# GpSimd handles both channel halves of a scan state in one instruction

## The reference

```
x = x + 0.5 * ffn(layernorm(x))     # 8 routed experts (top 2) + 2 shared experts
x = x + ssm(layernorm(x))           # selective state-space scan
x = x + 0.5 * ffn(layernorm(x))     # the same experts again
```

```
h[d,n] = exp(dt[d] * A[d,n]) * h[d,n] + dt[d] * B[n] * x[d]
y[d]   = sum over n of h[d,n] * C[n]  +  D[d] * x[d]
```

## Time and profile before

| | |
|---|---|
| three runs, us | 519.59, 522.36, 525.29 |
| span of the profiled execution (first to last instruction), us | 517.8 |
| VectorE busy, us | 324.0 (63%) |
| ScalarE busy, us | 158.6 (31%) |
| GpSimd busy, us | 231.4 (45%) |
| chain that ended last | PE 90%, DVE 6%, DMA 2% |
| scans with the tiles beside them | about 158 to 243 us and 296 to 380 us |

### The profile page before, as it was taken

The page is one execution under the profiler, slowest core; times in us unless marked ns, Lnnn a source line. Parts: engine busy times, 40 slices in busy tenths (PEclk is TensorE's granted clock), DMA queues, the critical chain, the costliest instruction groups (busy, mean ns, idle before and its releaser), DMA issues.

```text
span 517.8 us, 11713 instructions
## 1 busy us (share of the span) xinstructions
PE 506.7 (98%) x4666; PEld 423.2 (82%) x4667; DVE 324.0 (63%) x658; ACT 158.6 (31%) x337; POOL 231.4 (45%) x208
## 2 busy tenths in 40 slices
PE   8998999999999999999989999999999899999997
PEld 6998996568979999557979799975598899955696
DVE  3844338123747999997679399999967532422225
ACT  1111122221156434553203643445521111122210
POOL 1051000602216999995454289999920650000032
PEclk9999999999999999999999999999999999999999
DMA  7958999512415455541322445545200231210012
GB/s 231 392 231 303 394 389 346 178 59 66 129 36 142 118 139 135 163 117 30 113 63 71 129 94 121 156 131 155 73 22 2 72 101 52 82 42 14 20 54 81
DMA packets 42232, 67.91 MB, mean 131 GB/s; under 512 B 5152, under 2 KB 24992, under 8 KB 42176
## 3 DMA queue, kind: packets, MB, share of 16 engines
q1 hardware_dynamic: 29424, 38.94, 26.5%
q10 hardware_dynamic: 9088, 18.09, 9.4%
q0 software_dynamic: 3664, 10.10, 6.1%
HBM read 48.89 MB, written 18.22 MB: 130 GB/s over the span
## 4 chain that ended last, share of the span: by engine, by line
PE 90%; DVE 6%; DMA 2%; issue 1%; ACT 0%; POOL 0%; DVEq 0%; POOLq 0%; ACTq 0%
PE ps L526 40%; PE ps L551 20%; PE ps L541 14%; PE ps L564 7%; PE ps L570 2%; PE ps L575 2%; PE ps L707 2%; DMA bcb<-bc_rows 1%; PE ps L718 1%; PE ps L748 1%; DVE hb L1054 1%; DMA bc_rows<-hh 1%; DVE hb L1058 0%; PE ps L609 0%; PE ps L759 0%
## 5 line engine op out<-in xcount | busy, mean ns | idle before, releaser
L526 PEld LDWEIGHTS ps<-xt,w_gu 128*128 128x128 f32 x1400 | 161.6, 192 | 5.7 <-issue 3.8
L526 PE MATMUL ps<-xt,w_gu 128*128 128x128 f32 x1400 | 163.8, 276 | 0.4 <-DVE xres L1069 0.4
L1054 DVE SCALAR_TENSOR_TENSOR hb<-hb,ps 128x640 f32<-128x640 f32 x68 | 55.4, 815 | 121.3 <-ACT hb L800 121.2
L551 PE MATMUL ps<-w_dn,hb 128*128 128x256 f32 x520 | 120.8, 380 | 0.0
L551 PEld LDWEIGHTS ps<-w_dn,hb 128*128 128x128 f32 x520 | 94.8, 190 | 10.8
L800 ACT ACTIVATE hb<-ps 128x640 f32<-128x640 f32 x68 | 47.6, 700 | 176.9 <-PE ps L526 163.0
L526 PE MATMUL ps<-xnt,w_gu 128*128 128x128 f32 x680 | 80.5, 276 | 3.0 <-DVE xres L1069 2.7
L1099 DVE TENSOR_TENSOR_SCAN ps<-ps,region 128x512 f32<-128x512 f32 x64 | 78.3, 1223 | 8.1 <-POOL region L1018 6.2
L1032 POOL TENSOR_TENSOR xnt<-xnt,hh 128x512 f32<-128x512 f32 x64 | 82.2, 1286 | 2.5 <-DVE hh L1104 2.5
L526 PEld LDWEIGHTS ps<-xnt,w_gu 128*128 128x128 f32 x680 | 78.7, 192 | 5.5 <-DVE xres L1069 3.1
L998 POOL DMA_INDIRECT region<-yg_rows,ypos x32 | 30.5, 954 | 110.2 <-DMA yg_rows<-ob 88.4
(11 more groups left out here) (112 smaller groups left out, 302.0 us busy)
## 6 DMA issues: line engine op xcount, KB each, us to landing
bcb<-bc_rows SPq DMA_DIRECT2D x22, 512.0 KB, 5.1
region<-bc_rows SPq DMA_DIRECT2D x10, 512.0 KB, 5.0
w_gu<-in_wg ACTq DMA_DIRECT2D x7, 640.0 KB, 9.8
xg<-xg_rows SPq DMA_DIRECT2D x35, 128.0 KB, 4.2
w_gu<-in_wu ACTq DMA_DIRECT2D x7, 640.0 KB, 11.2
w_dn<-in_wd ACTq DMA_DIRECT2D x7, 640.0 KB, 13.8
yg_rows<-ob SPq DMA_DIRECT2D x20, 128.0 KB, 3.5
xg_rows<-bcb SPq DMA_DIRECT2D x1, 2176.0 KB, 14.9
```

The source lines that it names most:

```text
L526: last = nc.tensor.matmul(gup(p)[:, c * P:(c + 1) * P], w_gu4[:, e, k, c * P:(c + 1) * P], x, start=(k == 0), stop=(k == KC - 1))
L551: ins = nc.tensor.matmul(outp(p), hb[:, p, c * P:(c + 1) * P], w_dn4[:, e, c, :], start=(c == 0), stop=(c == IC - 1))
L1054: nc.vector.scalar_tensor_tensor(out=h, in0=h, scalar=1.0, in1=gup(p)[:, 0:I], op0=ALU.add, op1=ALU.mult).then_inc(s_a, 1)
```

## The change

GpSimd's two passes take both channel halves in one instruction of 128 partitions by 1024 elements: 16 inputs and 16 adds to a scan where there were 32 and 32. The input reads B once and spreads it over the two halves with a step of 0. bx exists twice, by even and odd state (the new one is `bx1`, 4 KB of each partition), and input m waits for the scans of state m-2. To make room, GpSimd's ring for DMA descriptors is set to 8 KB of each partition. VectorE's instructions stay as they are, 32 scans and 32 products; but a scan waits for the input of the whole state, and a product of state m for the add of the whole state m-1. TensorE's step Y counts 16 adds.

```diff
+        bx1 = sb("bx1", [P, KC, HALF])
...
-        bx = region[:, 1024:2048].rearrange("p (d t) -> p d t", d=KC)
+        bx = [region[:, 1024:2048].rearrange("p (d t) -> p d t", d=KC), bx1[:, :, :]]
...
-                    pe.wait_ge(s_acc, (h + 1) * HALVES)
+                    pe.wait_ge(s_acc, (h + 1) * N)
...
-                    def input_of(g):
-                        m, d = g // KC, g % KC
+                    def input_of(m):
                         pool.wait_ge(s_bcl[m % SLOTS], 16 * slot_loads(h, m))
-                        if m > 0:
-                            pool.wait_ge(s_scan, HALVES * h + g - KC + 1)
-                        nc.gpsimd.tensor_tensor(bx[:, d, :], dtx[:, d, :], bcs[m % SLOTS][:, 0, :],
-                                                ALU.mult).then_inc(s_bx, 1)
-
-                    for g in range(KC):
-                        pool.wait_ge(s_dtx, KC * h + g + 1)
-                        input_of(g)
-                    for g in range(HALVES):
-                        d = g % KC
-                        if g + KC < HALVES:
-                            input_of(g + KC)
-                        pool.wait_ge(s_hc, HALVES * h + g + 1)
-                        if g == 0:
+                        if m > 1:
+                            pool.wait_ge(s_scan, HALVES * h + KC * (m - 1))
+                        nc.gpsimd.tensor_tensor(bx[m % 2], dtx[:, :, :], bcs[m % SLOTS][:, 0:1, :]
+                                                .to_broadcast([P, KC, HALF]), ALU.mult).then_inc(s_bx, 1)
+
+                    pool.wait_ge(s_dtx, KC * (h + 1))
+                    input_of(0)
+                    input_of(1)
+                    for m in range(N):
+                        pool.wait_ge(s_hc, HALVES * h + KC * (m + 1))
+                        if m == 0:
                             pool.wait_ge(s_skip, h + 1)
-                        pool.wait_ge(s_acc, HALVES * h + max(g - KC + 1, 0))
-                        nc.gpsimd.tensor_tensor(xnt[:, d, :], xnt[:, d, :], hh[:, d, :], ALU.add).then_inc(s_acc, 1)
+                        else:
+                            pool.wait_ge(s_acc, N * h + m)
+                        nc.gpsimd.tensor_tensor(xnt[:, :, :], xnt[:, :, :], hh[:, :, :], ALU.add).then_inc(s_acc, 1)
+                        if m + 2 < N:
+                            input_of(m + 2)
...
-                    dve.wait_ge(s_bx, HALVES * h + g + 1)
-                    nc.vector.tensor_tensor_scan(state_banks[:, d, :], state_banks[:, d, :], bx[:, d, :], 0.0,
+                    dve.wait_ge(s_bx, N * h + m + 1)
+                    nc.vector.tensor_tensor_scan(state_banks[:, d, :], state_banks[:, d, :], bx[m % 2][:, d, :], 0.0,
...
                     if m > 0:
-                        dve.wait_ge(s_acc, HALVES * h + g - KC + 1)
+                        dve.wait_ge(s_acc, N * h + m)
...
-    nc = bacc.Bacc("TRN2", target_bir_lowering=False, num_devices=1)
+    nc = bacc.Bacc("TRN2", target_bir_lowering=False, num_devices=1, dynamic_dma_scratch_size=8192)
```

## The result

The change takes 548.39 us (median of 4 runs, 546.15 to 549.82), the kernel before in the same comparison 521.78 us (4 runs, 519.59 to 525.29): a ratio of 1.0511, 95% interval 1.0457 to 1.0565. The forecast was 549.4 us, range 541 to 556. The profiled execution took 546.15 us with a span of 544.2, 26.4 more than the span before.

A forecast was written before the change was run, and what follows sets the result against it. TensorE, busy 506.7 of 517.8 us, was taken as the bound; VectorE's new waits for whole adds, with start and end, make each scan 13.5 us longer, together +27.0 on the median 522.36: 549.4 us, range 541 to 556.

The forecast's parts named there:

- the named states: VectorE's product waits for the add before states 1, 2, 5, 6, 9, 10, 12, 13, 15: 13.1 us a scan.
- six covered: At six of 15 changes of state, a tile's hidden values stand between products on VectorE: no wait below T of 2.59.
- T: Time of a 1024-element GpSimd instruction, taken as 2.46 us; VectorE's wait without hidden values is T - 1.00.
- the sum: One scan's start, nine waits, exponentials' idle times and end: Y 13.5 us later, 11 us for each us of T.
- The later start: The first scan needs the input of both halves, so it starts at 160.42 instead of 159.23: +1.19 us.
- Y waits for the last add: At a scan's end TensorE reaches Y at about 255.2, but the last add lets Y start at 256.21.
- the ring: The smaller descriptor ring costs nothing: gathers start 1.25 us apart and land in 2.8, about three under way.
- the whole inputs and their step of 0: GpSimd's inputs between states cost nothing; the next add is held up only if an input takes over 2.7 us.
- the loads of B and C: Issued at the second product of m-1, landing 5.1 us later, needed over 7 us after it: no cost.
- A sign of being wrong that did show: The prediction is wrong if TensorE, now idle in places, is granted a clock of less than 1.00.
- Not slower: Rival: one GpSimd instruction is far cheaper than two, T below 1.47, at most +5.2 us for both scans; 6 in 100.
- slower still: Rival: GpSimd becomes the bound through slow inputs, or the halved ring holds gathers back: 556 us and more; 8 in 100.

The follow-up runs named there:

- run 5: The change with other shares of half-states to the 12 tiles: 546.58 us, the kernel before 525.52.
- run 8: The change with the input of state m+2 ahead of the add of state m on GpSimd's list: 590.71 us, the kernel before 525.52.
- run 4: The change with a second hh buffer, by even and odd state: 527.65 us, the kernel before 523.15.
- run 7: The change with adds as two instructions of 512, both behind both products of the state: 531.38 us, the kernel before 525.52.
- run 1: The kernel before with the descriptor ring at 8 KB and nothing else: 522.75 us, the kernel before 523.15.
- run 6: The kernel before with other shares of half-states to the 12 tiles: 535.07 us, the kernel before with its own shares 525.52.
- run 2: The change with adds by half, a product waiting for its own half's add, inputs whole: 524.95 us, the kernel before 523.15.
- run 9: The change with two hh buffers, and a scan's first input and last add in two instructions of 512: 523.48 us, the kernel before 522.71.
- run 3: The change with inputs in two instructions of 512, adds whole: 545.94 us, the kernel before 523.15.

## Why the prediction was right

- **Where the wait stands.** Nine in each scan, at the named states, six covered: seen in the change, and moved as forecast in runs 5 and 8. The step that carried the forecast, the add that begins only behind the product just before, is shown from both sides: doubling hh takes the waits away (run 4), a longer way to the release lengthens them by the amount worked out (run 8), a shorter one shortens them (run 7).
- **The size of a wait.** Forecast 1.46, measured 1.40. T was set at 2.46 us from twice the step of 1.23; the instruction takes 2.36. This is the term that was most off: the sum with 2.36 is 13.5 - 11 x 0.10 = 12.4 us a scan, measured 12.57 and 12.65. The estimate that the Trainium skill (GPSIMD Engine Reference, "Performance versus the Vector engine") gave, 2.34 from its 4497 ns for 2048 elements, was nearer, and the trace agrees with its price by the element: 1024 elements cost 1.09 us more than 512, where a quarter of 4497 ns is 1.12.
- **The total.** 12.57 + 12.65 = 25.2 of the 26.4 us between the spans. The other 1.16 lie ahead of the first scan, where the change has no part (run 1 shows 1.27 there with the ring alone, run 6 shows 3.7 with nothing edited ahead of the scan). Between the medians lie 26.6 us, 27.0 were forecast. So close a hit is partly luck: T was 0.10 too long, which makes 2.2 us for both scans, no term stood for the offset ahead of them, and executions of the kernel before alone lie 5.7 us apart.
- **Start and end.** The later start, forecast 1.19, was 1.09 (161.48 - 159.03 = 2.45 from input to scan, before 1.36). Y waits for the last add in both scans, 0.64 us, where the working had some 1.0.
- **Costed at nothing:** the ring (run 1), the whole inputs and their step of 0 (run 2), the loads of B and C, whose landings show up in the waits only at the scans' start. All held.
- **A sign of being wrong that did show.** The prediction names a granted clock below 1.00, and the sum has no term for it. In the profiled execution the clock fell for some 4 us in the second scan (last section), at hardly any cost that can be seen there. The four executions of the change had mean clocks of 0.996, 0.987, 1.000 and 0.990 and took 546.15, 549.82, 547.38 and 549.41 us, so in the others it may have cost some 3 us. The kernel before shows the same, so it doesn't speak against the wait for the add.
- **The rivals.** "Not slower" needed T below 1.47; "slower still" an input above 2.7 us or a full ring. Both are excluded by the rows: T is 2.34 to 2.40 us in all 64 instructions, and the last gathers of the change start 1.25 us apart, as before.

## What to carry to other kernels

Merging two instructions halves the number of handshakes but makes each one wait for more: what a waiting engine feels is the time from the last thing the merged instruction needs to its end, so look for how much of the waiter's own work lies in between, place by place in its list. If the merged instruction is what frees a buffer that exists once, double that buffer together with the merge: here this took away 10.5 of 12.65 us a scan (run 4). The change doubled bx, for which only GpSimd had waited (for scans of VectorE, 5.6 us in the whole run before), and not hh. And an engine that is 93% busy in a stage, as GpSimd was in the scans before, isn't a bound while the engine that sets the end is hardly ever idle: 4 us a scan saved on GpSimd were worth nothing (run 9).

## What the runs showed of the hardware

An instruction of 1024 elements with two inputs took GpSimd 2.34 to 2.40 us, whether one input had a step of 0 or not, where two of 512 took 2.49 together; back to back the steps from start to start are 2.32 and 2.46 us.

TensorE's granted clock, 1.00 in all windows of the kernel before in its profiled execution, dipped once in the second scan of the change. The windows of the change around it (columns as above):

```profile
374.00:376.00 2.00, 0.00 (x0) 0.00 (x0) 1.97 (x4) 0.78 (x2) 1.60 (x2) 1.00 0.13 48
376.00:378.00 2.00, 1.93 (x11) 1.46 (x15) 1.97 (x4) 0.08 (x1) 2.00 (x2) 0.56 0.78 164
378.00:380.00 2.00, 2.00 (x16) 0.46 (x12) 1.97 (x3) 1.32 (x3) 1.36 (x2) 0.59 0.55 181
380.00:382.00 2.00, 2.00 (x40) 1.02 (x36) 0.89 (x1) 0.98 (x2) 2.00 (x1) 1.00 0.50 102
```

TensorE had stopped for 1.49 us before 371.85 and for 2.29 us before 376.07; then for some 4 us the grant is near one half, the level of 1.2 GHz. The same pair of stops in the first scan (1.52 before 222.20, 2.29 before 226.42) brought no dip, the window of that scan reads 1.00. The dip cost hardly anything that can be seen: at the next hidden values, where TensorE waited 0.98 us in the first scan, it didn't wait in the second, and from the first input to Y the second scan lost 12.76 us where the first lost 12.57. In run 6 the same happened after one stop: 1.90 us before 179.79 in the first scan brought no dip, 1.90 before 321.96 in the second was followed by 4 us at 0.55 to 0.59. In run 8, with stops of up to 4 us, the mean clock was 0.976. What decides whether a stop is followed by a dip stays open.

The kernel before isn't free of this in other executions. Of the 19 beside runs 1 to 4, seven had a mean clock of 0.999 or 1.000 and took 519.50 to 521.24 us, four had 0.996 or 0.997 and took 521.31 to 523.98, and eight had 0.993 and took 524.73 to 526.04. So most of the 6.5 us between executions of one kernel goes with the granted clock; no trace shows where in the program those executions lost it.
